# Graph network on one core: units 14 and 15 of each set turned by VectorE in blocks and carried through DRAM

## The chip, the cores and the metric
One core of one Trainium2 chip. The metric is the device time of one execution in microseconds. Three runs of the kernel before took 1857.96, 1860.52 and 1862.22 us; the median is 1860.52.

## The reference
Four graph layers on 4096 nodes with 128 features, each followed by a residual and a layer norm. The change touches only the third, an attention over the whole graph with four heads of 32 features:

```python
q, k, v = [(x @ W + b).reshape(n, H, C) for ...]                  # H = 4, C = 32
attn = einsum('nhc,mhc->hnm', q, k) / sqrt(C)
neg = where(adj == 0, -inf, attn)
e = where(adj == 0, 0, exp(neg - max(neg)))
out = einsum('nhm,mhc->nhc', e / sum(e), v)                       # then gated with x @ Ws + bs
# layer 1: GRU(relu((adj @ x) @ W)), x        layer 2: normalised (adj + I) @ (x @ W)
# layer 4: hyperbolic: maps of x, adj @ xt, maps back
```

## The kernel before
Layers 1, 2 and 4 are products of the adjacency (64 MB) with a 4096 x 128 matrix. The adjacency streams through a ring of 8 slots of 1 MB (`ring`, `load_ring`); L446 is their matmul.

The attention layer works in **chunks** of 512 rows (8 of them, c = 0 to 7), each of four **tiles** of 128 rows, each of two **sets** of 2048 columns. A chunk has thus 8 sets, numbered 0 to 7 here, and a set 16 **units** of 128 columns; the 128 units of a chunk are also its **places** k. For each unit all four heads are handled together. The mask is made in **columns** of 1024 (16 in a chunk, two in a set). The steps:

- SyncE loads half a column of `adj` at a time into one of two landing tiles `adj_in` (`load_mask`, L345). The load of a half waits until GpSimd has used the same half of the column before.
- GpSimd makes -1e30 or 0 of it (`mask_bias`, L1360), at the earliest when VectorE is done with the column four back, six columns ahead of the place counter.
- TensorE makes scores, two matmuls of 512 columns for one head of one column (`scores`, L553), at every even place.
- VectorE scales, adds the mask and takes the minimum in one instruction (`mask`, L1109), at every odd place. The score banks are two, so a score waits for the mask two before it, and a mask of a new column waits for `unit_turned`: TensorE must be past the units that the tile `cols` still holds.
- ScalarE takes the exponent of one head of one set (`exponent`, L807).
- TensorE turns a unit, four 128 x 128 transposes into one of three PSUM banks (`turn_unit`, L580), at every place.
- ScalarE or VectorE copies it to one of 8 slots `turned` (`copy_unit`, L819 or L1124). VECTOR_PLACES, VECTOR_ALSO and VECTOR_NOT say which units VectorE takes (43 of 128), EXP_MOVED where exponents stand between the copies.
- TensorE multiplies it with the values (`attend`, L594), four units at once, seven places behind: the batch after place 3 of a set takes units 12 to 15 of the set before.

Between these lie post steps for the chunk before (`post_steps`: gate, norms and the hyperbolic maps of the next layer) at fixed places, on VectorE, ScalarE and GpSimd. On GpSimd a slot is four places; the norms wait for VectorE's place 77 (the reduction L1185). They exist in chunks 1 to 7, and mask bias calls end in chunk 7 with column 15. Each engine runs its own list in order, and each wait blocks all that is behind it, on SyncE's queue of DMAs too.

Every second set TensorE also turns the finished output of a tile (`turn_out`, L602, after place 6); at places 57 and 65 it does two steps for the chunk before. The next layer's ring loads (`load_ring(2, 0, True)`, L328) stand in SyncE's queue behind the attention's, and four of its slots lie over the first half of `cols`, four over the second.

## Time and profile before

| | |
|---|---|
| median of 3 runs | 1860.52 us |
| profiled execution, its own time | 1859.99 us |
| its span, first to last instruction | 1858.3 us |
| TensorE busy | 1805.1 us, 97% |
| VectorE busy | 1229.1 us, 66% |
| ScalarE busy | 983.0 us, 53% |
| GpSimd busy | 925.3 us, 50% |
| mean granted clock of TensorE | 0.987 |

The shares are averages over four layers. In the adjacency products TensorE and the DMA engines work and the rest mostly waits; the attention runs from about 590 to 1611 us and uses all engines. Each instruction has a start and a duration; TensorE's and VectorE's instructions overlap a little with the next, so what one costs is best read from start to start. Two fp32 records stand for each attend and each ring matmul.

### The profile page before, as it was taken

To read this page: it belongs to the slowest core of one execution; us is meant where nothing else is said; L and a number is where in the kernel's file an instruction comes from. 1 tells how busy PE (TensorE), PEld (TensorE's weight loads), DVE (VectorE), ACT (ScalarE), POOL (GpSimd) and SP (SyncE) were. 2 spreads that over 40 slices of the span, in tenths; PEclk is the share of its full clock that TensorE was granted. 3 is DMA by queue.
4 is the path that set the end of the run, shared out by engine and by line. 5 is a ranking of instruction groups with operands and counts; after the bars stand their busy time and mean duration, and the time that the engine had idled before them with its cause. 6 is when DMAs were issued, how large, how long until landed. Compare 5 with 4: busy or idle time off the path is not lost.

```text
span 1858.3 us, 41304 instructions
## 1 busy us (share of the span) xinstructions
PE 1805.1 (97%) x15504; PEld 1215.9 (65%) x15504; DVE 1229.1 (66%) x2398; ACT 983.0 (53%) x1512; POOL 925.3 (50%) x981
## 2 busy tenths in 40 slices
PE   7999999999996999999999999999999999999996
PEld 3444444444444888888888888888888888644442
DVE  4777775122226888898888888888988889401322
ACT  0111110101004888888888888988888988501101
POOL 0111111111225756778788788787787886540211
PEclk9999999999997999999999999999999999999998
DMA  9867767799977322213222222232133231697781
GB/s 376 303 227 260 256 225 251 270 391 380 400 271 220 93 91 72 83 58 95 88 73 90 74 82 86 70 92 91 60 93 93 64 96 49 242 356 281 281 325 71
DMA packets 110305, 328.82 MB, mean 177 GB/s; under 512 B 13104, under 2 KB 31280, under 8 KB 85552
## 3 DMA queue, kind: packets, MB, share of 16 engines
q1 hardware_dynamic: 87552, 285.25, 43.9%
q10 hardware_dynamic: 20016, 32.78, 4.9%
q0 software_dynamic: 2560, 8.39, 1.6%
q8 instruction: 115, 1.88, 0.4%
q14 instruction: 62, 0.51, 0.1%
HBM read 299.11 MB, written 27.26 MB: 176 GB/s over the span
## 4 chain that ended last, share of the span: by engine, by line
PE 59%; issue 3%; ACT 2%; POOL 2%; DVE 1%; POOLq 0%; DVEq 0%; ACTq 0%
PE bank L580 21%; PE bank L553 13%; PE bank L594 13%; PE bank L446 11%; ACT arena L807 2%; POOL arena L1360 1%; DVE arena L1124 1%; PE bank L434 0%; ACT L858 0%; PE bank L622 0%; PE bank L690 0%; POOL small L1480 0%; ACT arena L819 0%; PE bank L602 0%; POOL small L1367 0%
## 5 line engine op out<-in xcount | busy, mean ns | idle before, releaser
L580 PE MATMUL bank<-ident,arena 128*128 128x128 f32 x4096 | 540.0, 274 | 5.4 <-ACT arena L807 2.4
L580 PEld LDWEIGHTS bank<-ident,arena 128*128 128x128 f32 x4096 | 478.1, 141 | 82.5 <-DVE arena L1124 7.7
L807 ACT ACTIVATE arena<-arena,small 128x2048 f32<-128x2048 f32 x256 | 512.5, 2002 | 0.1
L819 ACT ACTIVATE arena<-bank 128x512 f32<-128x512 f32 x680 | 382.4, 596 | 125.3 <-PE bank L580 123.0
L446 PE MATMUL bank<-arena,stat_s 128*128 128x512 f32 x1008 | 441.4, 595 | 2.1 <-issue 1.2
L553 PE MATMUL bank<-k,parts 128*128 128x512 f32 x1024 | 371.8, 445 | 13.3 <-DVE small L1109 7.0
L446 PEld LDWEIGHTS bank<-arena,stat_s 128*128 128x128 f32 x1008 | 190.2, 191 | 228.3 <-issue 226.9
L1124 DVE COPY arena<-bank 128x512 f32<-128x512 f32 x344 | 236.7, 688 | 73.3 <-PE bank L580 71.6
L1360 POOL TENSOR_SCALAR early<-arena 128x512 bf16<-128x512 f32 x128 | 246.3, 1925 | 68.9 <-DVE small L1109 26.7
L594 PE MATMUL bank<-arena,stat_x 128*32 128x128 f32 x8192 | 276.5, 276 | 0.0
L1360 POOL TENSOR_SCALAR arena<-arena 128x512 bf16<-128x512 f32 x128 | 247.2, 1931 | 40.5 <-DVE small L1109 19.8
L446 PE MATMUL bank<-arena,stat_x 128*128 128x512 f32 x512 | 229.2, 599 | 10.7 <-DMA arena<-adj_cols 8.5
L594 PEld LDWEIGHTS bank<-arena,stat_x 128*32 128x32 f32 x8192 | 208.1, 109 | 42.8 <-issue 42.8
L553 PEld LDWEIGHTS bank<-k,parts 128*128 128x128 f32 x1024 | 155.6, 191 | 68.0 <-issue 44.2
L446 PEld LDWEIGHTS bank<-arena,stat_x 128*128 128x128 f32 x512 | 96.4, 192 | 125.7 <-issue 125.4
L1109 DVE CUSTOM_DVE_ANT_0 arena<-bank,early,small 128x1024 f32<-128x1024 f32 x128 | 163.5, 1279 | 16.6 <-issue 9.3
L1109 DVE CUSTOM_DVE_ANT_0 arena<-bank,arena 128x1024 f32<-128x1024 f32 x128 | 155.9, 1219 | 26.2 <-PE bank L580 20.9
L1109 DVE CUSTOM_DVE_ANT_0 arena<-bank,arena,small 128x1024 f32<-128x1024 f32 x128 | 163.2, 1277 | 6.2 <-issue 5.2
L1109 DVE CUSTOM_DVE_ANT_0 arena<-bank,early 128x1024 f32<-128x1024 f32 x128 | 155.8, 1218 | 15.0 <-PE bank L553 7.8
L1305 POOL TENSOR_SCALAR small<-small 128x4 f32<-128x4 f32 x32 | 13.0, 407 | 251.5 <-DVE small L937 251.5
L1367 POOL TENSOR_TENSOR small<-small 128x4 f32<-128x4 f32 x160 | 78.8, 492 | 60.5 <-DVE small L1185 35.8
L1367 POOL TENSOR_TENSOR arena<-arena 128x512 f32<-128x512 f32 x64 | 76.3, 1192 | 36.4 <-ACT arena L848 20.7
(152 smaller groups left out, 1182.8 us busy)
## 6 DMA issues: line engine op xcount, KB each, us to landing
arena<-adj_cols SPq DMA_DIRECT2D x190, 1024.0 KB, 6.3
arena<-adj SPq DMA_DIRECT2D x256, 256.0 KB, 2.7
k_dram<-arena ACTq DMA_DIRECT2D x32, 256.0 KB, 6.7
q_dram<-arena ACTq DMA_DIRECT2D x32, 256.0 KB, 11.7
k<-k_dram POOLq DMA_DIRECT2D x32, 256.0 KB, 8.5
parts<-q_dram SPq DMA_DIRECT2D x128, 64.0 KB, 2.3
x_dram<-arena ACTq DMA_DIRECT2D x16, 256.0 KB, 3.6
arena<-x_dram ACTq DMA_DIRECT2D x16, 256.0 KB, 4.9
```

The source lines that it names most:

```text
L446: mm_ = pe.matmul(bank[:, to, :], stat[:, jt, :], ring[:, s, j, :], start=(jt == 0), stop=(jt == TILES - 1))
L553: last = pe.matmul(bank[:, u + i, :], parts[:, t % 2, h * P:(h + 1) * P], k4[:, h, at_:at_ + CHUNK], start=True, stop=True)
L580: last = pe.transpose(bank[:, b_, h * P:(h + 1) * P], cols[:, st % SETS, h, u * P:(u + 1) * P], ident[:, :])
L594: last = pe.matmul(bank[h * C:(h + 1) * C, 7, st * P:(st + 1) * P], stat_x[:, k % UPT, h * C:(h + 1) * C], turned[k % TURNED][:, h * P:(h ...
L807: act.activation(cols[:, s_, h, :], cols[:, s_, h, :], ACT.Exp, bias=shift[:, t % 2, 1, i:i + 1], scale=-1.0, accum_out=blocksum[:, t % 2, ...
L819: act.activation(turned[k % TURNED], bank[:, TURN_BANKS.bank(("unit", k)), :], ACT.Copy).then_inc(unit_copied_act, 1)
L1109: dve.tensor_tensor_reduce(out=cols[:, s_, h, hi * BLOCK:(hi + 1) * BLOCK], in0=bank[:, 2 * (h % 2):2 * (h % 2) + 2, :].rearrange("p b n - ...
L1124: dve.tensor_copy(turned[k % TURNED], bank[:, TURN_BANKS.bank(("unit", k)), :]).then_inc(unit_copied_dve, 1)
L1305: step(c, "eps", pool.tensor_scalar(rstd, mean_var[:, :, 1], LN_EPS, None, ALU.add))
L1360: pool.tensor_scalar(maskbias[m % 4][:, e * HALF:(e + 1) * HALF], adj_in[e], 0.0, MASKED, ALU.is_equal, ALU.mult).then_inc(bias_ready, 1)
L1367: step(c, name, pool.tensor_tensor(out_, a, b, op))
```

## The change
Units 14 and 15 of each set (`PAIRS`) are not turned by TensorE. VectorE turns them in 32 x 32 blocks (`turn_blocks`, at places 4 and 7 of the set) into `pair_blocks`, eight tiles of `stat_s`, which the next layer fills only later. SyncE stores the 512 KB to one of two DRAM buffers (`store_pair`) and loads them with four DMAs of 128 KB, which put the blocks in place (`load_pair`), into slots 6 and 7 of the ring of turned units. The attend of such a unit waits for `pair_landed` and reads its operand in runs of 32 elements. The mask loads are named six columns ahead (`MASK_AHEAD`), which places them between the stores and loads of the pairs; the residual loads move to the end of a chunk. VectorE's copies are 32 a chunk, ScalarE's 80, at other places.

```diff
+BLOCK_TURN_AT = {14: 4, 15: 7}
+PAIRS = ((14, 15),)
+VECTOR_PLACES = ()
+VECTOR_ALSO = (0, 4, 8, 11, 13, 16, 20, 23, 24, 34, 54, 58, 64, 67, 73, 83, 85, 86, 88, 90, 92, 98, 102, 104, 105, 106, 113, 115, 118, 121, 123, 125)
...
+MASK_AHEAD = 6
...
+    pair_dram = nc.dram_tensor("pair_dram", [2, P, 2 * CHUNK], F32)
...
+        pair_slot = arena[:, RING + 10 * CHUNK:RING + 12 * CHUNK]
+        pair_blocks = stat_s[:, TILES - 2 * TPC:TILES, :].rearrange("p t f -> p (t f)")
...
                     if first and layer == 2 and s % 4 == 0:
-                        sp.wait_ge(unit_turned, (CHUNKS * SPC - 2 + s // 4 + 1) * UPS)
+                        turned_before = (CHUNKS * SPC - 2 + s // 4 + 1) * UPS
+                        sp.wait_ge(unit_turned, pe_turns(turned_before))
+                        sp.wait_ge(blocks_turned, block_turns(turned_before))
...
+            def store_pair(g):
+
+                i = pairs_until(g)
+                sp.wait_ge(blocks_turned, 2 * (i + 1))
+                if i >= 2:
+                    sp.wait_ge(pair_landed, 16 * (P // C) * (i - 1))
+                sp.dma_start(pair_dram[i % 2, :, :], pair_blocks).then_inc(pair_out, 16)
+
+            def load_pair(g):
+
+                i = pairs_until(g)
+                sp.wait_ge(pair_out, 16 * (i + 1))
+                if i == 0:
+                    sp.wait_ge(gcn_x2_out, 16 * CHUNKS)
+                if g + 1 >= TURNED:
+                    sp.wait_ge(unit_used, g + 1 - TURNED + 1)
+                for j in range(P // C):
+                    sp.dma_start(pair_slot[j * C:(j + 1) * C, :].rearrange("k (q n) -> k q n", q=P // C),
+                                 pair_dram[i % 2, :, j * 2 * P:(j + 1) * 2 * P].rearrange("(q k) n -> k q n", q=P // C)
+                                 ).then_inc(pair_landed, 16)
+
+            def attention_loads(c):
+                for st in range(SPC):
+                    for half_set in range(2):
+                        ahead = c * COLS + 2 * st + half_set + MASK_AHEAD
+                        if ahead < CHUNKS * COLS:
+                            load_mask(ahead // COLS, ahead % COLS, False)
+                        for pair in PAIRS:
+                            if pair[0] // UPB == half_set:
+                                store_pair(c * UPC + st * UPS + pair[0])
+                        if half_set == 1 and st % SETS == 1:
+                            ahead = c * TPC + st // SETS + 2
+                            if ahead < CHUNKS * TPC:
+                                load_queries(ahead // TPC, ahead % TPC, False)
+                        if half_set == 1 and st == 4 and c > 0:
+                            store_x3(c - 1)
+                        for pair in PAIRS:
+                            if pair[0] // UPB == half_set:
+                                load_pair(c * UPC + st * UPS + pair[0])
+                load_residuals(c)
...
+                if is_block_turned(k):
+                    pe.wait_ge(pair_landed, 16 * (P // C) * (pairs_until(c * UPC + k) + 1))
...
-                    turn_unit(c, k, first)
+                    if not is_block_turned(k):
+                        turn_unit(c, k, first)
...
+            def turn_blocks(c, k):
+
+                st, u = k // UPS, k % UPS
+                i = pairs_until(c * UPC + k)
+                dve.wait_ge(exp_ready, (c * SPC + st) * H + H)
+                if i > 0:
+                    dve.wait_ge(pair_out, 16 * i)
+                dve.transpose(pair_tiles(pair_blocks)[:, in_pair(k), :, :, :],
+                              cols[:, st % SETS, :, u * P:(u + 1) * P].rearrange("p h (j k) -> p h j k", j=P // C)
+                              ).then_inc(blocks_turned, 1)
...
+                    if isinstance(c, int) and c == CHUNKS - 2:
+                        pool.wait_ge(pair_out, 16 * CHUNKS * SPC * len(PAIRS))
                     tt("xt", stat_s[:, bass.ds(c * TPC, TPC), :], tiles(mx_g), s1.unsqueeze(2).to_broadcast([P, TPC, P]),
```

`pairs_until(g)`, `pe_turns(g)` and `block_turns(g)` count the pairs, the units turned by TensorE and the block turns before unit g of the layer. On **TensorE**, the last eight places of a set before:

```order
L553 MATMUL bank<-k,parts 128x512 x2
L580 MATMUL bank<-ident,arena 128x128 x8
L553 MATMUL bank<-k,parts 128x512 x2
L580 MATMUL bank<-ident,arena 128x128 x8
L594 MATMUL bank<-arena,stat_x 32x128 x16
```

and the same places now (L618 scores, L645 turns, L667 attend), with the first scores of the next set:

```order
L618 MATMUL bank<-k,parts 128x512 x2
L645 MATMUL bank<-ident,arena 128x128 x8
L618 MATMUL bank<-k,parts 128x512 x2
L645 MATMUL bank<-ident,arena 128x128 x8
L667 MATMUL bank<-arena,stat_x 32x128 x16
L618 MATMUL bank<-k,parts 128x512 x2
L645 MATMUL bank<-ident,arena 128x128 x8
L618 MATMUL bank<-k,parts 128x512 x2
L667 MATMUL bank<-arena,stat_x 32x128 x16
L618 MATMUL bank<-k,parts 128x512 x2
```

The eight turns between the last scores of a set and its last attend are gone. On **SyncE**, in the middle of the layer before (L345 mask halves, L354 queries, L374 and L375 residuals):

```order
L345 DMA arena<-adj 128x512 [waits bias_ready] x8
L354 DMA parts<-q_dram 32x4x128 [waits scores_ready]
L354 DMA parts<-q_dram 32x4x128 x3
L345 DMA arena<-adj 128x512 [waits bias_ready] x4
L374 DMA arena<-x_dram 128x512 [waits att_x3_out,att_pool]
L375 DMA arena<-root_dram 128x512
```

and now, one set of the even kind and one of the odd (L387 mask halves, L406 store of the pair, L417 its loads, L396 queries):

```order
L387 DMA arena<-adj 128x512 [waits bias_ready] x4
L406 DMA pair_dram<-stat_s 128x1024 [waits pair_landed,blocks_turned]
L417 DMA arena<-pair_dram 32x4x256 [waits unit_used,pair_out]
L417 DMA arena<-pair_dram 32x4x256 x3
L387 DMA arena<-adj 128x512 [waits bias_ready] x4
L406 DMA pair_dram<-stat_s 128x1024 [waits pair_landed,blocks_turned]
L396 DMA parts<-q_dram 32x4x128 [waits scores_ready]
L396 DMA parts<-q_dram 32x4x128 x3
L417 DMA arena<-pair_dram 32x4x256 [waits unit_used,pair_out]
L417 DMA arena<-pair_dram 32x4x256 x3
```

Each set's store has four mask halves ahead of it, and the next set's mask halves have the pair's loads ahead of them. On **VectorE**, places 2 to 8 of set 2 before (L1109 masks, L1124 copies, L1142 the weighing of an output):

```order
L1124 COPY arena<-bank 128x512 [waits unit_used,unit_turned]
L1109 ISA arena,small<-bank,early,small 128x1024 [waits masked_ready,scores_ready]
L1109 ISA small 128x1
L1109 ISA arena,small<-bank,early,small 128x1024 [waits masked_ready,scores_ready]
L1109 ISA small 128x1
L1124 COPY arena<-bank 128x512 [waits unit_used,unit_turned]
L1109 ISA arena,small<-bank,arena 128x1024 [waits scores_ready,bias_ready,unit_turned]
L1109 ISA small 128x1
L1142 TENSOR_TENSOR arena<-bank,small 128x256 [waits rows_pe,rows_pool]
```

and now (L1182 masks, L1197 copies, L1206 block turns, L1226 the weighing):

```order
L1197 COPY arena<-bank 128x512 [waits unit_used,unit_turned]
L1182 ISA arena,small<-bank,early,small 128x1024 [waits masked_ready,scores_ready]
L1182 ISA small 128x1
L1206 STREAM_TRANSPOSE stat_s<-arena 128x4x4x32 [waits pair_out,exp_ready]
L1182 ISA arena,small<-bank,early,small 128x1024 [waits masked_ready,scores_ready]
L1182 ISA small 128x1
L1182 ISA arena,small<-bank,arena 128x1024 [waits scores_ready,blocks_turned,bias_ready,unit_turned]
L1182 ISA small 128x1
L1206 STREAM_TRANSPOSE stat_s<-arena 128x4x4x32 [waits pair_out,exp_ready]
L1226 TENSOR_TENSOR arena<-bank,small 128x256 [waits rows_pe,rows_pool]
```

One block turn comes before the mask of place 5, one behind the mask of place 7; the copy of place 6 is gone from VectorE.

## Rows read from the trace of the kernel before

**Rows 1.** Windows (length, then PE, PEld, DVE, ACT, POOL busy): sets 4 to 7, 0

```profile
1038.61:1055.25 16.64, 16.64 (x223) 14.12 (x219) 14.36 (x28) 14.72 (x23) 9.52 (x7) 1.00 0.35 105
1055.25:1070.80 15.55, 15.55 (x213) 13.01 (x209) 14.96 (x26) 13.36 (x19) 12.65 (x20) 1.00 0.12 35
1070.80:1087.46 16.66, 16.22 (x214) 13.09 (x210) 14.19 (x26) 15.43 (x24) 13.65 (x22) 1.00 0.27 81
1087.46:1102.99 15.53, 15.53 (x212) 12.99 (x208) 13.42 (x23) 13.85 (x22) 13.48 (x15) 1.00 0.26 79
1102.99:1119.25 16.26, 16.17 (x215) 13.19 (x211) 13.84 (x26) 13.94 (x21) 13.79 (x12) 1.00 0.40 122
...
sum 127.99, PE 127.45 PEld 106.01 DVE 113.12 ACT 113.14 POOL 101.71; mean PE 15.93 PEld 13.25 DVE 14.14 ACT 14.14 POOL 12.71
```

**Rows 2.** Timeline (start, us, engine, line) of TensorE: places 0 to 3 of set 7

```profile
1086.45 1.08 PE L594 MATMUL bank<-arena,stat_x 128*32 128x128 f32 x32
1087.46 0.73 PE L553 MATMUL bank<-k,parts 128*128 128x512 f32 x2
1088.03 1.03 PE L580 MATMUL bank<-ident,arena 128*128 128x128 f32 x8
1088.82 0.71 PE L553 MATMUL bank<-k,parts 128*128 128x512 f32 x2
1089.37 1.04 PE L580 MATMUL bank<-ident,arena 128*128 128x128 f32 x8
1090.33 1.08 PE L594 MATMUL bank<-arena,stat_x 128*32 128x128 f32 x32
```

**Rows 3.** Timeline of VectorE: a copy and the mask behind it

```profile
1065.64 0.68 DVE L1124 COPY arena<-bank 128x512 f32<-128x512 f32 x1
1066.24 1.21 DVE L1109 CUSTOM_DVE_ANT_0 arena<-bank,early 128x1024 f32<-128x1024 f32 x1
```

**Rows 4.** Timeline of VectorE at place 7 of set 6; TensorE's attend batch then

```profile
1078.89 1.22 DVE L1109 CUSTOM_DVE_ANT_0 arena<-bank,arena 128x1024 f32<-128x1024 f32 x1 [0.84 <-PE bank L580]
1080.04 0.42 DVE L1142 TENSOR_TENSOR arena<-bank,small 128x256 f32<-128x256 f32 x1
...
1078.69 1.08 PE L594 MATMUL bank<-arena,stat_x 128*32 128x128 f32 x32
```

**Rows 5.** SyncE's DMAs: queries, to landing; then x_dram, to landing

```profile
L354 SPq DMA_DIRECT2D parts<-q_dram x120: 327/432/1577, 606.1 to 1528.8; - x120
...
DMA to landing us min/median/max: 1.9/2.3/3.9
...
DMA to landing us min/median/max: 2.8/3.3/4.7
```

**Rows 6.** Landing times of mask halves (256 KB), then of ring slots (1 MB)

```profile
DMA to landing us min/median/max: 2.5/2.7/4.6
...
DMA to landing us min/median/max: 4.7/6.7/12.1
```

**Rows 7.** Timeline of GpSimd: the norms, then biases of sets 5, 6, 7, 0

```profile
1055.09 1.04 POOL L1367 TENSOR_TENSOR small<-small 128x4 f32<-128x4 f32 x1 [5.00 <-DVE small L1185]
...
1060.23 3.94 POOL L1360 TENSOR_SCALAR arena<-arena 128x512 bf16<-128x512 f32 x2 [0.25 <-POOL small L1367]
...
1080.11 3.94 POOL L1360 TENSOR_SCALAR early<-arena 128x512 bf16<-128x512 f32 x2 [0.25 <-POOL small L1367]
...
1096.46 3.94 POOL L1360 TENSOR_SCALAR arena<-arena 128x512 bf16<-128x512 f32 x2 [0.25 <-POOL small L1367]
...
1109.94 3.93 POOL L1360 TENSOR_SCALAR early<-arena 128x512 bf16<-128x512 f32 x2 [0.25 <-POOL stat_s L1367]
```

**Rows 8.** Timeline of TensorE: place 8 of the layer's last set; the next product

```profile
1604.08 2.00 PE L580 MATMUL bank<-ident,arena 128*128 128x128 f32 x16
...
1610.93 3.70 PE L446 MATMUL bank<-arena,stat_s 128*128 128x512 f32 x8
```

More of the change, by code:

```diff
@@ L100, in __call__, with is_block_turned, pe_turns, pairs_until @@
         return c * len(self.names) + self.names.index(name) + 1
+def is_block_turned(k):
+    return k % UPS in BLOCK_TURN_AT
+PE_UNITS = [k for k in range(UPC) if not is_block_turned(k)]
+def pe_turns(g):
+    return g // UPC * len(PE_UNITS) + sum(k < g % UPC for k in PE_UNITS)
+def pairs_until(g):
+    return g // UPS * len(PAIRS) + sum(pair[-1] < g % UPS for pair in PAIRS)
+def block_turns(g):
+    return g // UPS * len(BLOCK_TURN_AT) + sum(u < g % UPS for u in BLOCK_TURN_AT)
+def in_pair(k):
+    return [pair.index(k % UPS) for pair in PAIRS if k % UPS in pair][0]
 class TurnBanks:
@@ L111, in __init__ @@
         for k in range(UPC):
-            self.uses.append(("unit", k))
+            if not is_block_turned(k):
+                self.uses.append(("unit", k))
             if k % UPT == OUT_AT:
@@ L141 @@
 LAST_BLOCK_CHUNK = CHUNKS - BLOCK // CHUNK
-BY_VECTOR = [k for k in range(UPC) if (k % 16 in VECTOR_PLACES or k in VECTOR_ALSO) and k not in VECTOR_NOT]
-BY_SCALAR = [k for k in range(UPC) if k not in BY_VECTOR]
+BY_VECTOR = [k for k in PE_UNITS if (k % 16 in VECTOR_PLACES or k in VECTOR_ALSO) and k not in VECTOR_NOT]
+BY_SCALAR = [k for k in PE_UNITS if k not in BY_VECTOR]
 EXP_PLACES = [EXP_MOVED.get(k, k) for k in range(1, UPC, 4)]
@@ L356, in load_queries @@
                                  ).then_inc(q4_landed[t % 2], 16)
-            def attention_loads(c, first):
-                for m in range(COLS):
-                    if m % BLOCKS == 0:
-                        load_queries(c, m // BLOCKS, first)
-                    if not (first and m == 0):
-                        load_mask(c, m, first)
-                    if m == 5 and not first:
-                        load_residuals(c - 1)
-                    if m == 15 and not first:
-                        store_x3(c - 1)
@@ L372, in load_residuals @@
+            def load_residuals(c):
+                if c == 0:
+                    sp.wait_ge(gcn_q_out, 64 * CHUNKS)
+                    sp.wait_ge(gcn_root_out, 16 * CHUNKS)
+                    sp.wait_ge(gcn_x2_out, 16 * CHUNKS)
+                else:
                     sp.wait_ge(att_pool, AG(c - 1, "h"))
@@ L1211, in attention @@
                         below_max(c, k // UPT)
+                    for u, place in BLOCK_TURN_AT.items():
+                        if k % UPS == place:
+                            turn_blocks(c, k - place + u)
                     if k in BY_VECTOR:
```

55 lines of the change are left out of this document (27 added, 28 removed).

## The prediction
> **What bounds the kernel now.** I read the table of windows first, one window for each set of the middle chunks. TensorE is busy in 127.45 of 127.99 us of a chunk at full clock; VectorE has 113.12, ScalarE 113.14, GpSimd 101.71 [rows 1]. So in the attention layer (eight such chunks of the 1858.3 us span) TensorE is the bound and the other two stand at 88%. Then the timeline of TensorE, which repeats every 3.88 us: two scores, 8 turns, two scores, 8 turns, one attend batch [rows 2]. From the second 8 turns to the attend is 0.96 us, the attend batch 1.01 us, a pair of scores 0.54 to 0.57 us, and a plain set 4 x 3.88 = 15.5 us. A turn is thus 0.11 to 0.12 us of TensorE. Last I read VectorE around place 7 of a set, GpSimd from place 77 to the end of a chunk, and the landing times of SyncE's transfers, because the new transfers wait in SyncE's queue behind mask loads, which wait for GpSimd.
>
> **What TensorE loses.** Units 14 and 15 of each of 64 sets are no longer turned: 8 turns a set. Bounds: 0.79 us (the first 8 turns of a period) to 0.96 us (the second) [rows 2]; I take 0.93, since the removed ones stand where the 0.96 is. That is 7.4 us a chunk, 59.5 in all (51 to 62), if nothing else is late.
>
> **VectorE and ScalarE.** VectorE makes 32 copies a chunk instead of 43 and 16 block turns; ScalarE 80 copies instead of 85, so it only gets lighter. A copy holds VectorE for 0.60 us, start to start [rows 3]. No block turn is in the trace. It moves as many elements (512 a partition) as a copy, so I take 0.65, just above that row; the ends are 0.5 and 1.15, the mask of 1024 elements [rows 4]. VectorE: 113.1 - 11 x 0.60 + 16 x 0.65 = 116.9 us, against 119.5 that TensorE would need (below). It fits on the whole but not in each set: set 6 goes from 14.19 to 15.5 (five copies stay, two turns come), set 7 from 13.42 to 15.3 (one copy more, two turns), where a set of TensorE is 14.6 to 15.0. In the other sets copies go where the turns come. I charge about 1 us a chunk for this.
>
> The Trainium skill (VectorE: DVE Perf Modes, The three transpose paths) gives 311 ns for a 128x128 bf16 block turn; four of them would be 1.24 us, an estimate by that page. Its DVE Microarchitecture page (The reshape front-end and per-opcode configuration) says the transposing array keeps one element per cycle per lane, which would put it at the copy. No run here shows either; my sum goes by the copy, and the slow case is a rival below.
>
> **The round trip of the pair.** Store 512 KB, wait, load 4 x 128 KB. Rows: 256 KB to and from DRAM land in 3.3 us, mask halves of 256 KB in 2.7, queries of 64 KB in 2.3, ring slots of 1 MB in 6.7 among others and 4.7 at best [rows 5, 6]. From 2.7 to 4.7 is 2.0 us for 768 KB more, so 256 KB more cost 0.65 and the store 3.3 + 0.65 = 3.95. The four loads issue 0.43 us apart, so the last is out after 1.3 us and lands 2.4 later (between 64 and 256 KB): 3.7. With 0.4 for two semaphores and the transfers beside: 8.1 us. Bounds: (2.8 + 0.65) + (1.0 + 1.9) = 6.4 with each at its best, (4.7 + 0.65) + (1.3 + 3.9) + 0.2 = 10.7 with each at its slowest [rows 5].
>
> The time it has: the mask of place 7 begins at 1078.89 and lets the next instruction go at 1080.04; TensorE's place 8 began at 1078.69 + 1.01 = 1079.70. So the block turn of place 7 ends 0.34 + 0.65 = 1.0 us into place 8 [rows 4]. Place 8 to place 16 is 7.76, less 0.93; from place 16 to the attend batch 2.87, and unit 14 stands in its middle, 0.5 later [rows 2]. That gives 6.83 + 3.37 - 1.0 = 9.2 us, against 8.1. In a plain set the trip is hidden with 1.1 us to spare.
>
> The Trainium skill (DMA: Bandwidth & Descriptors, Anatomy of one DMA) puts a transfer at 2.0 us plus bytes over 436 GB/s. For 256 KB that is 2.6 us; the mask half's 2.7 agrees [rows 6], the 3.3 of the transfers with DRAM buffers does not [rows 5]. By the rule the trip would be some 7 us and the waits below 1 us a trip shorter.
>
> **The step I think decides: SyncE's order.** Its queue is now, for each set, mask load of column 2s+6, mask load of column 2s+7, store, pair loads. The second half of the load of column 2s+7 waits until GpSimd has finished both halves of the bias of column 2s+6. In the kernel before such a load could be late at no cost; now the store stands behind it. Where does GpSimd finish that bias, counted from the start of the set on TensorE? Set 5 (start 1055.25): 1064.2, 8.9 us in, just in time, for VectorE's turn ends 9 to 10 us in. Set 6 (start 1070.80): 1080.11 + 3.94 = 1084.05, 13.3 us in. Set 7 (1087.46): 1100.40, 12.9 us in. Set 0 (1102.99): 1113.87, 10.9 us in [rows 1, 7]. GpSimd hardly idles from 1055.09 on, where the norms of place 77 begin after a wait of 5.0 us for VectorE; from there to the end of set 6's bias are 29.0 us of its own work, and that does not shrink.
>
> One chunk after, time from the start of set 4: sets 4, 5, 6 take 15.7, 14.6 and 15.0 (before less 0.93; set 6 also loses waits, [rows 1]). Norms begin at 16.5, set 6's bias is done at 45.5, the store goes at 45.9, the pair is there at 54.0. TensorE wants it at 15.7 + 14.6 + 15.0 + 3.4 = 48.7: it waits 5.3 us, in set 7. Next: bias of set 7 done at 61.8, pair at 70.3, wanted at 45.3 + 5.3 + 14.6 + 3.4 = 68.6: 1.7 us more. Set 0's bias, at 75.3, is then earlier than VectorE's turn. So 7.0 us a chunk. The wait also lets VectorE catch up in sets 6 and 7. The eight sets less 0.93 each, without the old waits of sets 6 and 0 (1.1), are 119.5; 119.5 + 7.0 + 0.5 = 127.0, a gain of 1 us, with a little taken for the uneven start 1.3. This holds for chunks 1 to 6. Chunk 0 has no post steps on GpSimd, chunk 7 loads no masks from set 5 on: 7.4 - 1 = 6.4 each.
>
> **Edits priced at nothing.** Mask loads named six columns ahead still find only two landing tiles, so they run one column ahead of GpSimd as before; after the pair loads the even column's load goes out some 14.9 us into a set and lands 2.7 later, 3 us into the next. In sets 5 to 0 GpSimd comes to it later than that; in sets 3 and 4 it may be ready before, and its 5.0 us of waiting ahead of the norms take that up [rows 7]. Query loads, the residual loads and the store of x3 sit in the 4 us in which SyncE waits for the store anyway; each has over 10 us until it is wanted. The attend of a block-turned unit reads runs of 32 elements and not 128: same number of columns, taken at the same 1.01 us a batch (a slower read would show in that batch). The wait of GpSimd in the last chunk for all stores stands ahead of nothing that TensorE wants before the sixth slot of the next layer.
>
> **The end of the layer.** The next layer's product starts at 1610.93 with its first four slots loaded since the second last set was turned [rows 8]. Now its loads stand behind the last pair. Place 8 of the last set is at 1604.08 [rows 8]; with no mask ahead of it the last block turn is done by about 1603.8. The store lands at 1607.9, the loads are out by 1609.6, the two residual loads by 1610.4, then slot 0 of 1 MB takes 4.7 to 6.7 [rows 6]. The product starts at 1615.1 to 1617.1 instead of 1610.0 (a set's 0.93 less): 6 us lost (3 to 9). Later slots come faster (2.6 us a MB) than TensorE takes them (8 records in 3.7 us).
>
> **Sum.** 6 x 1.3 + 2 x 6.4 - 6 = 14.6 us faster. The profiled execution took 1859.99 us (span 1858.3 and 1.7 around it), 0.5 less than the median of the runs, 1860.52. So 1859.99 - 14.6 = 1845.4, with the half microsecond to the median 1846 us. Own range of this case 1830 to 1862: a microsecond in the round trip moves it by some 1.5 us a chunk.
>
> **Rivals.**
> A. SyncE's order costs nothing, because GpSimd runs ahead when TensorE is late, or the trip is short. For it: GpSimd has 101.7 us of work in 127. Against: it is without a pause exactly where the store waits. Then 59.5 - 8 (VectorE) - 6 = 45.5: 1814.5, as a run 1815 us.
> B. The block turn costs 1.15 us instead of 0.65: VectorE has 125 us a chunk, with its issue gaps about 127, and is the bound: 8 x 1 - 6 = 2, so 1858 us. For it: the page's figure. Against: nothing in these rows.
> C. Slower. The trip outlasts its 9.2 us in every set, so place 3 of each set waits. It decides from 9.2 us on, and the gain is gone from about 9.5. At 10 us, six plain sets pay 0.8 each (4.8) and the two late ones 7.5: 131.8 us a chunk, 3.8 more than now. 6 x 3.8 = 23, chunks 0 and 7 gain 1 each, and the end costs 6: 27 slower, 1887 us; with every transfer at its slowest 1925. For it: transfers of one set overlap mask and query loads. Against: the medians leave 1.1 us.
>
> **Chances.** Forecast 0.47, A 0.17, B 0.11, C 0.25. A difference under 0.2% (1856.8 to 1864.2) can't be told from none. Of the forecast's case four fifths lie below that band and an eighth in it; A is all faster; B is half in it; C is slower. Faster 0.58, same 0.11, slower 0.31. The range goes from A's time to C's at 10 us, a microsecond beyond each: 1814 to 1888.
>
> **What would show it.** TensorE's attend batch at place 3 of a set waits for a transfer: about 5 us in set 7, 2 in set 0, nothing in sets 2 to 5. The store's issue follows the mask load at once in sets 6 and 7, and VectorE's turn elsewhere. Block turn 0.65 us (B: over 1). Store plus loads 8.1 us (C: over 9.2, a wait in all sets). The ring loads start after the last pair load. I am wrong if place 3 waits nowhere, or everywhere.

## The result, and the profile after

| | before | after |
|---|---|---|
| median of the runs | 1860.71 us (6 runs) | 1874.44 us (6 runs, 1871.91 to 1882.83) |
| profiled execution | 1859.99 us, span 1858.3 | 1871.91 us, span 1870.2 |
| mean granted clock of TensorE | 0.987 | 0.982 |

The kernel became slower: the ratio is 1.0082, with an interval of 1.0060 to 1.0104. The forecast was 1846 us, so the direction was missed. The range of 1814 to 1888 held the time, but the forecast's own range ended at 1862; the wider one reached up to the time of a rival whose cause did not occur.

The windows of sets 4 to 7 and 0 of a middle chunk of the kernel after, with the columns of [rows 1]:

```profile
1168.10:1184.34 16.24, 16.00 (x214) 13.11 (x210) 15.01 (x29) 14.61 (x23) 11.15 (x8) 1.00 0.40 130
1184.34:1199.01 14.67, 14.67 (x204) 12.06 (x200) 14.32 (x25) 13.91 (x23) 11.77 (x20) 1.00 0.49 155
1199.01:1214.57 15.56, 15.31 (x206) 12.17 (x203) 14.93 (x30) 14.64 (x21) 12.71 (x21) 1.00 0.29 90
1214.57:1234.69 20.12, 16.37 (x205) 13.13 (x201) 15.29 (x26) 12.56 (x18) 17.53 (x18) 0.92 0.48 154
1234.69:1252.02 17.33, 15.31 (x207) 12.20 (x203) 14.65 (x28) 13.04 (x18) 12.24 (x10) 1.00 0.51 162
```

Set 5 is 0.9 us shorter than before (14.67 for 15.55), set 6 1.1. Set 7 is 4.6 us longer, and in it the granted clock is 0.92, GpSimd busy for 17.53 us. Set 0 is 1.1 longer.

Inside set 7, the timeline of TensorE at places 2 and 3, to be read beside [rows 2]:

```profile
1215.93 0.71 PE L618 MATMUL bank<-k,parts 128*128 128x512 f32 x2
1216.47 1.03 PE L645 MATMUL bank<-ident,arena 128*128 128x128 f32 x8
1217.44 0.64 PE L667 MATMUL bank<-arena,stat_x 128*32 128x128 f32 x16
1221.83 1.08 PE L667 MATMUL bank<-arena,stat_x 128*32 128x128 f32 x16 [3.75 <-DMA arena<-pair_dram]
1222.84 1.22 PE L618 MATMUL bank<-k,parts 128*128 128x512 f32 x2
1223.86 1.65 PE L645 MATMUL bank<-ident,arena 128*128 128x128 f32 x8
1225.27 0.70 PE L618 MATMUL bank<-k,parts 128*128 128x512 f32 x2
```

The batch stops after units 12 and 13 and waits 3.75 us for the pair. Behind the wait the same instructions take longer: scores 1.22 for 0.71 us, eight turns 1.65 for 1.03, the half batch 1.08 for 0.64. The windows of these stretches give the clock, the third column from the right:

```profile
1221.83:1225.20 3.37, 3.37 (x25) 2.66 (x26) 1.00 (x1) 0.24 (x1) 2.83 (x5) 0.51 0.38 120
1225.20:1230.66 5.46, 5.46 (x65) 4.53 (x63) 4.50 (x10) 5.27 (x9) 4.67 (x6) 1.00 0.21 57
```

The granted clock is 0.51, the lower level of 1.2 GHz, for these 3.4 us, then 1.00 again. It costs half the stretch, about 1.7 us, on top of the wait.

Why the pair is late: SyncE's queue, and the biases of GpSimd (start, us), in the same sets; they answer to [rows 7]:

```profile
1197.75 1.74 SPq L417 DMA_DIRECT2D arena<-pair_dram  x4
1200.73 12.84 SPq L387 DMA_DIRECT2D arena<-adj  x4
1213.67 0.38 SPq L406 DMA_DIRECT2D pair_dram<-stat_s  x1
1217.63 1.75 SPq L417 DMA_DIRECT2D arena<-pair_dram  x4
...
1198.75 3.95 POOL L1447 TENSOR_SCALAR arena<-arena 128x512 bf16<-128x512 f32 x2 [0.25 <-POOL small L1454]
1209.27 3.94 POOL L1447 TENSOR_SCALAR early<-arena 128x512 bf16<-128x512 f32 x2 [0.25 <-POOL small L1454]
1218.38 3.92 POOL L1447 TENSOR_SCALAR early<-arena 128x512 bf16<-128x512 f32 x2 [0.25 <-POOL arena L1454]
```

The four mask halves leave over 12.84 us, the last when GpSimd's bias of 1209.27 ends at 1213.21. The store is out 0.46 later, the loads 3.96 behind it, and the pair is there at 1221.83.

VectorE's block turn, beside the copy and mask of [rows 3, 4]:

```profile
1595.53 0.68 DVE L1197 COPY arena<-bank 128x512 f32<-128x512 f32 x1
1596.13 0.70 DVE L1206 STREAM_TRANSPOSE stat_s<-arena 128x512 f32<-128x512 f32 x1
1596.76 0.38 DVE L1226 TENSOR_TENSOR arena<-bank,small 128x256 f32<-128x256 f32 x1
```

It holds VectorE 0.63 us, start to start; a copy 0.60.

The end of the layer, to be read with [rows 8]:

```profile
1612.89 1.52 PE L667 MATMUL bank<-arena,stat_x 128*32 128x128 f32 x48
1618.66 1.08 PE L667 MATMUL bank<-arena,stat_x 128*32 128x128 f32 x16 [4.25 <-DMA arena<-pair_dram]
1623.22 5.99 PE L511 MATMUL bank<-arena,stat_s 128*128 128x512 f32 x8 [3.48 <-DMA arena<-adj_cols]
```

The last pair comes 4.25 us late, the first ring slot 3.48 later still, and the first eight records of the product take 5.99 us for 3.70. From the start of the layer's last set to the product are 20.65 us, 13.28 before.

**Where the time went.** Differences between the two profiled executions, beside the terms of the prediction, in us; the 0.9 that the last set was to gain stands with the end (6 - 0.9), where it was measured:

| part | predicted | measured |
|---|---|---|
| chunk 0, to its end | -6.4 | -1.0 |
| chunks 1 to 6 | -7.8 | +7.7 |
| chunk 7, sets 0 to 6 | -5.5 | -1.8 |
| last set and end of the layer | +5.1 | +7.4 |
| the rest | 0 | -0.4 |
| sum | -14.6 | +11.9 |

The six chunks took 128.1, 129.5, 128.3, 131.2, 129.8 and 129.3 us, 129.4 in the mean, against 128.0 to 128.4 before. In set 7 TensorE waited for the pair 3.84, 4.26, 1.66, 3.75, 3.87 and 2.76 us, in set 0 0.34 to 1.77: 4.5 a chunk. The low clock followed in set 7 of all but the third of them, and in set 1 of chunk 0 behind a wait of 2.45.

### The profile page after: what moved, and what is told of

It reads as the page before. It is cut to its first block and busy times, and to the rows that moved or that the text cites. A ratio compares the mean times of both kernels' runs of the same rounds, so it can differ in the third digit from the quotient of the medians.

```text
span 1870.2 us, 40787 instructions
## 1 busy us (share of the span) xinstructions
PE 1767.1 (94%) x14992; PEld 1160.7 (62%) x14992; DVE 1253.1 (67%) x2438; ACT 965.8 (52%) x1472; POOL 925.4 (49%) x981
## 5 line engine op out<-in xcount | busy, mean ns | idle before, releaser
L645 PE MATMUL bank<-ident,arena 128*128 128x128 f32 x3584 | 481.6, 275 | 7.7 <-DVE arena L1226 7.3
L645 PEld LDWEIGHTS bank<-ident,arena 128*128 128x128 f32 x3584 | 422.3, 142 | 79.3 <-DVE arena L1226 14.5
L891 ACT ACTIVATE arena<-bank 128x512 f32<-128x512 f32 x640 | 358.2, 598 | 115.4 <-PE bank L645 112.5
L618 PE MATMUL bank<-k,parts 128*128 128x512 f32 x1024 | 375.2, 449 | 15.2 <-DVE small L1182 8.5
L667 PE MATMUL bank<-arena,stat_x 128*32 128x128 f32 x8192 | 284.1, 278 | 38.2 <-DMA arena<-pair_dram 38.1
L667 PEld LDWEIGHTS bank<-arena,stat_x 128*32 128x32 f32 x8192 | 208.1, 110 | 99.4 <-issue 49.2
L1197 DVE COPY arena<-bank 128x512 f32<-128x512 f32 x256 | 173.5, 686 | 49.6 <-PE bank L645 49.0
L618 PEld LDWEIGHTS bank<-k,parts 128*128 128x128 f32 x1024 | 156.8, 193 | 72.3 <-issue 44.0
L1182 DVE CUSTOM_DVE_ANT_0 arena<-bank,arena,small 128x1024 f32<-128x1024 f32 x128 | 161.1, 1277 | 22.0 <-issue 21.0
L1182 DVE CUSTOM_DVE_ANT_0 arena<-bank,early,small 128x1024 f32<-128x1024 f32 x128 | 162.0, 1275 | 12.8 <-PE bank L618 7.7
L1182 DVE CUSTOM_DVE_ANT_0 arena<-bank,arena 128x1024 f32<-128x1024 f32 x128 | 155.1, 1217 | 19.9 <-PE bank L645 9.8
L1182 DVE CUSTOM_DVE_ANT_0 arena<-bank,early 128x1024 f32<-128x1024 f32 x128 | 154.9, 1215 | 5.5 <-PE bank L618 5.2
L1206 DVE STREAM_TRANSPOSE stat_s<-arena 128x512 f32<-128x512 f32 x128 | 90.2, 705 | 0.0
## 6 DMA issues: line engine op xcount, KB each, us to landing
arena<-pair_dram SPq DMA_DIRECT2D x256, 128.0 KB, 2.8
```

The source lines that it names most:

```text
L618: last = pe.matmul(bank[:, u + i, :], parts[:, t % 2, h * P:(h + 1) * P], k4[:, h, at_:at_ + CHUNK], start=True, stop=True)
L645: last = pe.transpose(bank[:, b_, h * P:(h + 1) * P], cols[:, st % SETS, h, u * P:(u + 1) * P], ident[:, :])
L667: last = pe.matmul(to, stat_x[:, k % UPT, h * C:(h + 1) * C], weights, start=(u == 0), stop=(u == UPS - 1))
L891: act.activation(turned[k % TURNED], bank[:, TURN_BANKS.bank(("unit", k)), :], ACT.Copy).then_inc(unit_copied_act, 1)
L1182: dve.tensor_tensor_reduce(out=cols[:, s_, h, hi * BLOCK:(hi + 1) * BLOCK], in0=bank[:, 2 * (h % 2):2 * (h % 2) + 2, :].rearrange("p b n - ...
L1197: dve.tensor_copy(turned[k % TURNED], bank[:, TURN_BANKS.bank(("unit", k)), :]).then_inc(unit_copied_dve, 1)
```

## The experiments

Two theories stood at the start. One is the prediction's: the pair is late because SyncE's queue makes its store wait for mask loads, and these for GpSimd. The other: it is late because of VectorE's turn, or the trip itself. Times are medians, each ratio is to the kernel before with its 95% interval; the kernel after stands at 1874.44 us. Lines headed by what waits and for what are totals of waits (us, times, longest) from 700 to 1560 us.

**e1_store_first.** The store ahead of the mask load of the odd column.

```diff
-                        if ahead < CHUNKS * COLS:
-                            load_mask(ahead // COLS, ahead % COLS, False)
...
                                 store_pair(c * UPC + st * UPS + pair[0])
+                        if ahead < CHUNKS * COLS:
+                            load_mask(ahead // COLS, ahead % COLS, False)
```

> Only SyncE's order changes: in each set the store of the pair stands ahead of the mask load of column 2s+7, not behind it. Theory Q (the store is late because it queues behind a mask load that waits for GpSimd): the store goes when VectorE's second block turn is done in all sets, the pair loads of sets 6 and 7 are at most half a microsecond late, set 7 falls from about 20.1 us to 15, set 0 by about 1.5, and the stretches at half clock behind those waits go too: about 7 us a chunk in chunks 1 to 6, so 1828 to 1838 us. Rival T (store plus loads are simply longer than the time they have): the waits in sets 7 and 0 stay, above 1860 us.

Measured: 1903.0 us, 1.0229 (1.0201 to 1.0258). The expectation failed.

```profile
SPq L406 <- DVE stat_s L1206: 283.8, 52, 9.6
...
POOL early L1447 <- DMA arena<-adj: 62.4, 25, 6.5
...
PE bank L667 <- DMA arena<-pair_dram: 31.7, 17, 4.2
```

The store now waits for VectorE's turn at the head of the queue, 283.8 us (32.5 in the kernel after), and the mask load behind it goes out late. GpSimd waits 62.4 us for mask halves ahead of the biases into `early` and 84.8 in all, for 67.6 in all in the kernel after, and VectorE waits for GpSimd's post steps in set 2, which takes 17 to 19 us for 15.35. The coupling was turned round, not removed, and TensorE waits 31.7 us for the pair as in the kernel after (31.4).

**e2_mask_last.** Store, pair loads, and only then the odd column's mask load.

```diff
-                        if ahead < CHUNKS * COLS:
+                        if half_set == 0 and ahead < CHUNKS * COLS:
...
                                 load_pair(c * UPC + st * UPS + pair[0])
+                        if half_set == 1 and ahead < CHUNKS * COLS:
+                            load_mask(ahead // COLS, ahead % COLS, False)
```

> SyncE's order again: store, pair loads, and only then the mask load of column 2s+7. Theory Q: no wait for the pair in any set. If GpSimd has slack enough, the time is that of the variant with the store first, 1828 to 1838 us. Rival P (GpSimd is the hidden bound): its column 2s+7 now comes late in every set, it waits for mask halves, the masks of VectorE come late in sets 6 and 7, and the time is 5 to 20 us above the variant with the store first.

Measured: 1966.58 us, 1.0576 (1.0556 to 1.0596). From 700 to 1560 us TensorE waits for no pair any more (one wait of 3.9 us is left, at the end of the layer), and the masks became the bound:

```profile
PE bank L621 <- DVE small L1185: 62.1, 20, 6.8
...
POOL arena L1450 <- DMA arena<-adj: 65.5, 16, 8.7
...
DVE small L1005 <- POOL arena L1457: 46.1, 6, 8.2
```

The expectation's rival, late masks and a late GpSimd, had the kind and was far too low in size. The masks have no slack to give to the pair.

**e3_turn_early.** The block turns at places 2 and 5 instead of 4 and 7.

```diff
-BLOCK_TURN_AT = {14: 4, 15: 7}
+BLOCK_TURN_AT = {14: 2, 15: 5}
```

> VectorE's block turns at places 2 and 5 of a set in place of 4 and 7. SyncE's order stays. Theory Q: the store of sets 6 and 7 waits for GpSimd, not for VectorE, so set 7 stays near 20.1 us. The even sets lose the 0.5 us that the weighing behind the turn of place 7 costs: 4 x 0.5 x 8 = 16 at most, so 1860 to 1868 us. Rival T: the trip starts 1.8 us earlier, so the wait in set 7 falls from 3.8 to 2.0 and that in set 0 goes: 1845 to 1855 us.

Measured: 1872.22 us, 1.0058 (1.0036 to 1.0080).

```profile
SPq L406 <- DVE stat_s L1206: 2.0, 3, 0.8
...
PE bank L667 <- DMA arena<-pair_dram: 32.5, 20, 4.8
```

The store no longer waits for VectorE (2.0 us for 32.5), and TensorE waits for the pair as long as before (32.5 for 31.4). So VectorE's turn is not what makes the pair late. A by-product: sets 2, 3, 4 and 6 fall by 0.3 to 0.45 us (set 2 from 15.35 to 15.05). In the kernel after TensorE waits 26 times for the weighing (L1226), 6.4 us, and 7 times for the normalising in VectorE's post steps (L1018), 3.9 us; the turn at place 7 stands just ahead of the weighing. In e3 neither wait is left.

**e4_no_trip.** Neither store nor loads; the attend reads VectorE's tile as it stands, so the blocks are not in their places and the output is not the reference's. The turn, which waited for the store before, now waits until TensorE has used the pair before (not in the cut below).

```diff
             def store_pair(g):
-                sp.dma_start(pair_dram[i % 2, :, :], pair_blocks).then_inc(pair_out, 16)
+                return
...
-                    pe.wait_ge(pair_landed, 16 * (P // C) * (pairs_until(c * UPC + k) + 1))
+                    pe.wait_ge(blocks_turned, 2 * (pairs_until(c * UPC + k) + 1))
...
-                        weights = pair_tiles(pair_slot)[:, in_pair(k), h, :, :]
+                        weights = pair_tiles(pair_blocks)[:, in_pair(k), h, :, :]
```

> No store and no loads of the pair: the attend of units 14 and 15 reads VectorE's block-turned tile directly, so its blocks are not in their places and the output is not the reference's. It prices what is left without the trip. Theory Q plus VectorE's price as the sets without a wait show it (14.66 odd, 15.35, 15.88, 16.24, 15.57 the even ones and set 3): about 122.8 us a chunk in place of 128.0, no late ring loads: 1815 to 1822 us. Rival B (VectorE's turns are the bound): above 1850 us.

Measured: 1838.15 us, 0.9885 (0.9866 to 0.9905), some 20 us above what was expected. Chunks 0 and 1 were near the forecast; from chunk 2 on set 2 took 17.4 to 19.3 us instead of 15.35, and a chunk 125.7 to 127.7.

```profile
DVE small L989 <- POOL arena L1441: 22.0, 6, 4.6
```

In set 2 VectorE waits for GpSimd's post steps, 4.6 us at most. A second bound was hidden under the first: GpSimd, whose post steps VectorE needs (e6 tests it).

**e5_light_pool** and **e6_no_trip_light.** The kernel after, and e4, with a GpSimd whose biases cost 1.07 us a half instead of 1.93, because from chunk 1 on they make only half of the mask (the output is not the reference's).

```diff
-                    pool.tensor_scalar(maskbias[m % 4][:, e * HALF:(e + 1) * HALF], adj_in[e], 0.0, MASKED,
-                                       ALU.is_equal, ALU.mult).then_inc(bias_ready, 1)
+                    width = HALF if is_zero(c) else HALF // 2
+                    pool.tensor_scalar(maskbias[m % 4][:, e * HALF:e * HALF + width], adj_in[e][:, 0:width], 0.0,
+                                       MASKED, ALU.is_equal, ALU.mult).then_inc(bias_ready, 1)
```

> The changed kernel with less work on GpSimd: from chunk 1 on each mask bias call handles 256 of its 512 columns (the other half keeps an older bias, so the output is not the reference's). Order and transfers are the same. Theory G (GpSimd's late bias holds the store in SyncE's queue, and GpSimd's chain is the second bound): set 7 falls from 20.1 us to 15, set 0 to 15.4, no half clock behind them: about 123 us a chunk in chunks 1 to 6, 1825 to 1840 us. Rival T (the round trip itself is too long): set 7 stays at 19 or more, 1865 to 1875 us.

> Both at once: no round trip (the attend reads the block-turned tile) and half the mask bias on GpSimd; output not the reference's. Theory G: the 17.5 to 18.8 us of set 2 in the kernel without the trip are VectorE waiting for GpSimd's blend; they fall to 15.4, a chunk to about 123, and the time from 1838 to 1815 to 1824 us. Rival V (VectorE's own work makes set 2 long): no change, 1833 to 1841 us.

Measured: e5 1842.83 us, 0.9906 (0.9878 to 0.9934); e6 1817.38 us, 0.9764 (0.9744 to 0.9783). e6 is where its theory had it, e5 3 us above its bounds and far from the rival.

```profile
PE bank L667 <- DMA arena<-pair_dram: 6.1, 6, 2.0
```

With the whole trip in place but a lighter GpSimd, the wait for the pair in e5 is 6.1 us instead of 31.4, and set 7 takes 14.9 to 15.2. The waits fall by 25.3 us, and one stretch of low clock is left of five in chunks 1 to 6; at about 1.6 us each that makes 31.7 by estimate, and the whole gain is 31.6. In e6 every middle chunk takes 123.1 to 123.4 us. That is the kernel's speed without pair waits, and 3.2 above the 120.0 that the prediction had for it (119.5 and 0.5).

**e10_before_light.** The control: the same lighter biases in the kernel before, same diff.

> Control: the kernel before, with the mask bias on GpSimd computed over half its width from chunk 1 on (output not the reference's), as in the run with light biases of the kernel after. Theory G (GpSimd's lateness costs only where the pair's store or the masks wait for it, that is in the kernel after): the kernel before had 0.5 and 0.6 us of waits in set 6 and set 0 of a chunk that led back to masks, so at most 7 x 1.1 = 8 us go: 1852 to 1860 us. Rival H (the light biases gain as much in any kernel, some 30 us as in the kernel after, so that run said nothing of the pair): about 1830 us.

Measured: 1857.37 us, 0.9981 (0.9969 to 0.9993). It is worth 0.19% there, 3.5 us, and 31.6 us in the kernel after (1874.44 less 1842.83). A chunk takes 127.4 us there instead of 128.0. GpSimd's lateness was nearly free before and is paid where the pair stands behind it in the queue.

**e7_act_store.** ScalarE issues the store, at place 10, past SyncE's queue.

```diff
-                                store_pair(c * UPC + st * UPS + pair[0])
...
+                    if k % UPS == STORE_AT:
+                        store_pair(c * UPC + k - STORE_AT + PAIRS[0][0])
```

> The pair's store is issued by ScalarE at place 10 of the set; mask loads, queries and pair loads stay in SyncE's queue in the same order. Theory G: the store no longer waits for the mask loads; in sets 6 and 7 the pair loads still wait for them until 13.7 us into the set, which is just in time. Set 7 falls from 20.1 to 15 to 16 us, but GpSimd's blend then holds set 2 (16 to 18 us): 1840 to 1852 us. Rival: ScalarE, held by the wait at place 10 and 0.4 us of issue a set, becomes late: above 1870 us.

Measured: 1873.35 us, 1.0063 (1.0043 to 1.0083); missed. Set 7 fell to 15.1 to 16.0 in chunks 1 to 6, and set 0 rose to 18.4 to 22.8 from chunk 2 on.

```profile
1090.05 9.59 SPq L388 DMA_DIRECT2D arena<-adj  x4
1099.68 2.46 SPq L397 DMA_DIRECT2D parts<-q_dram  x4
1102.24 1.80 SPq L410 DMA_DIRECT2D arena<-pair_dram  x4
...
1095.34 3.94 POOL L1447 TENSOR_SCALAR arena<-arena 128x512 bf16<-128x512 f32 x2 [0.25 <-POOL small L1454]
...
SPq L408 <- PE bank L657: 129.2, 34, 6.2
...
POOL early L1447 <- DMA arena<-adj: 40.3, 24, 7.2
POOL arena L1447 <- DMA arena<-adj: 30.7, 16, 5.8
```

The pair loads still sit in SyncE's queue. The rows are sets 7 and 0 of a middle chunk: the store of set 7 has left at 1096.03, but its loads stand behind four mask halves that wait for GpSimd's bias (done at 1099.28) and behind the query loads, so they go out at 1102.24, and TensorE waits 2.77 us at place 3 of set 0. It is the same coupling, one set later and at the loads instead of the store. SyncE also waits longer for TensorE to free the pair's slots (129.2 us for 58.4), but GpSimd waits for masks hardly longer than in the kernel after (71.0 us for 67.6), so late masks do not explain the stall.

**e8_ring_early.** The first two ring slots of the next layer ahead of the last set's pair.

```diff
+                    if c == CHUNKS - 1 and st == SPC - 1:
+                        load_ring(2, 0, True, EARLY_SLOTS)
...
-            load_ring(2, 0, True)
+            load_ring(2, 0, True, SLOTS, EARLY_SLOTS)
```

> The kernel after, with one edit at the end of the attention layer: SyncE loads the first two ring slots of the next layer before the last set's masks, store and pair loads, and the other six behind them. In the kernel after, the next product starts 20.65 us after the start of set 63 on TensorE, 13.28 in the kernel before; of the 7.4 us between, 4.25 are the wait for the last pair, 3.48 the wait for the first ring slot behind it. Theory E (the end of the layer costs because the ring loads stand behind the last pair): the second wait goes, and part of the time at the lower clock behind it: 3.5 to 5 us less than the kernel after, 1869 to 1871 us. Rival R (the two early megabytes delay the last pair by as much as they save, since both share the same DMA engines): within 1.5 us of the kernel after, 1873 to 1876 us, with the wait for the pair in set 63 grown from 4.25 to about 8 us. The sets before 63 are as in the kernel after in both.

Measured: 1876.64 us, 1.0081 (1.0059 to 1.0103). The time points to the rival, the trace does not:

```profile
1623.16 1.08 PE L670 MATMUL bank<-arena,stat_x 128*32 128x128 f32 x16 [4.11 <-DMA arena<-pair_dram]
1624.17 6.18 PE L514 MATMUL bank<-arena,stat_s 128*128 128x512 f32 x8
```

The last pair's wait stays (4.11), the wait for the ring slot is gone, and the product starts 16.94 us after the last set instead of 20.65: 3.7 gained. They were lost in the attention, whose last set began at 1607.23 instead of 1602.57, with the same code up to there and a mean granted clock of 0.975 for 0.982. The six runs of the kernel after lie 10.9 us apart among themselves, so a gain of 3.7 at the end can't be read from the time of the whole; it is read from the trace.

**e11_half_turn.** e6 with VectorE's block turn over half the elements.

```diff
+                heads = H if is_zero(c) else H // 2
-                dve.transpose(pair_tiles(pair_blocks)[:, in_pair(k), :, :, :],
+                dve.transpose(pair_tiles(pair_blocks)[:, in_pair(k), 0:heads, :, :],
```

> The run without the trip and with light biases, and VectorE's block turns cut from 512 to 256 elements a partition from chunk 1 on (output not the reference's). That run took 1817.4 us with chunks of 123.1 to 123.4 us, where the prediction had 119.5 for TensorE alone plus 1 for VectorE. Theory V (the 3.6 us beyond are VectorE's: scores' masks and weighing wait behind the block turns in the even sets): 16 turns cheaper by about 0.3 us each let chunks fall by 1 to 2.5 us, 1800 to 1810 us. Rival W (what is left is TensorE's own, its periods saving 0.87 and not 0.93 us, and ScalarE's copies): chunks stay within 0.3 us of 123.2, 1815 to 1818 us.

Measured: 1812.84 us, 0.9736 (0.9719 to 0.9752): between the two.

```profile
L1194 DVE STREAM_TRANSPOSE stat_s<-arena 128x256 f32<-128x256 f32 x112 | 49.4, 441 | 4.7 <-PE bank L654 4.6
```

A half turn takes 441 ns for 705, 4.2 us less of VectorE a chunk, and a chunk falls from 123.2 to 122.4. Part of the 3.2 is thus VectorE's; this run shows 0.8, and twice that for the whole turn would be 1.6, an estimate.

**e9_all.** What helped, put together: store from ScalarE at place 8, turns at places 2 and 5, GpSimd's blend a slot earlier, two ring slots early.

```diff
-BLOCK_TURN_AT = {14: 4, 15: 7}
+BLOCK_TURN_AT = {14: 2, 15: 5}
+EARLY_SLOTS = 2
+STORE_AT = 8
...
-                return {4: beta_terms, 6: residual_terms, 9: blend, 11: rs, 14: x3sq, 17: mx_terms, 19: norms,
+                return {4: beta_terms, 6: residual_terms, 8: blend, 11: rs, 14: x3sq, 17: mx_terms, 19: norms,
```

> Four edits together: the store from ScalarE (place 8), block turns at places 2 and 5, GpSimd's blend one slot earlier (before a mask bias), and the first two ring slots of the next layer loaded ahead of the last pair. Theory G: waits in sets 7, 0 and 2 mostly gone, the product of the next layer 5 us earlier: 1818 to 1835 us, below the kernel before. Rival: GpSimd's total chain (its mask loads come behind the pair loads) still holds the chunk at 126 us or more: 1845 to 1860 us.

Measured: 1852.75 us, 0.9950 (0.9930 to 0.9969): it beats both kernels, by less than expected. Sets 2 to 5 take 15.1, 15.4, 15.8 and 14.7 us, but set 0 17.2 to 21.3 from chunk 2 on. As in e7, the pair loads of set 7 stand behind mask halves that wait for GpSimd: in a middle chunk these leave from 1083.95 to 1093.55, the pair loads at 1096.32.

```profile
SPq L409 <- PE bank L660: 110.6, 42, 5.9
...
PE bank L660 <- DMA arena<-pair_dram: 24.9, 12, 3.7
```

**e12_act_both.** e9, with the pair loads on ScalarE too.

```diff
+                    if k % UPS == LOAD_AT:
+                        load_pair(c * UPC + k - LOAD_AT + PAIRS[0][0])
```

> The combination that beat both kernels at 1852.75 us (store issued by ScalarE at place 8, block turns at places 2 and 5, blend in slot 8, two early ring slots), and now the four pair loads are issued by ScalarE too, at place 13 of the set, so that no pair transfer stands in SyncE's queue behind a mask load, and no mask load behind a pair. The combination still had sets 0 at 17 to 21 us and sets 7 at 16 to 18, with pair loads behind mask loads. Theory S (what was left of the loss is the coupling in SyncE's queue): sets 7 and 0 fall to 15 to 16 us in chunks 1 to 7, chunks to 123 to 125, 1828 to 1840 us. Rival T (GpSimd is the second bound by itself: as soon as TensorE is faster than 125 us a chunk, masks come late whoever issues the pair): chunks 126 to 128, 1845 to 1855 us. Rival U (ScalarE's five issues a set and its wait for the store cost it what it has not: copies late, TensorE waits for ScalarE in each set): above 1860 us.

Measured: 1901.16 us, 1.0216 (1.0195 to 1.0238). The time is rival U's, above 1860, but TensorE waits for the pair and hardly for copies, so none of the three has the cause. SyncE's coupling did go: GpSimd waits 31.2 us in all for `adj`, for 67.6 in the kernel after. But the loads come late:

```profile
1118.20 0.34 ACTq L878 DMA_DIRECT2D pair_dram<-stat_s  x1
...
1127.29 2.01 ACT L857 ACTIVATE arena<-arena,small 128x2048 f32<-128x2048 f32 x1 [1.80 <-DVE small L1185]
1127.35 3.12 ACTq L889 DMA_DIRECT2D arena<-pair_dram  x4
```

They leave 9.15 us behind the store, where SyncE needed 3.96. ScalarE reaches its place 13 only behind exponents, one of which waits for a mask. TensorE waits for the pair 32 times, 41.3 us, from 700 to 1560 us, and 7.5 and 11.9 us at the end of the layer. An earlier place for the loads was not tried.

## Why the prediction was wrong

**Right: the path by which the pair comes late, nearly to the microsecond.** From the start of set 4 the prediction had the bias of set 6 done at 45.5, the store out at 45.9, the pair there at 54.0. Measured: 45.1, 45.6 and 53.7; the trip took 8.16 us for 8.1. The pair was wanted at 50.0 and not 48.7, because the three sets ahead took 46.5 us and not 45.3, so the wait was 3.75 and not 5.3. Bias of set 7 done at 61.5, forecast 61.8. The marks held in kind: waits in set 7 (1.66 to 4.26, forecast about 5), smaller ones in set 0 (0.34 to 1.77, forecast 2), the ring loads behind the last pair load. One held in part: 24 of the 53 stores from 700 to 1560 us waited for VectorE's turn, the store of set 5 in the chunk shown did not. e3, e5 and e10 together show the cause: not VectorE's turn and not the length of the trip, but GpSimd through the mask loads. The stall was forecast at 7.0 a chunk; it measured 4.5, and with the clock 5.9.

**Right: the turns and the size of the block turn.** Plain sets such as set 5 became 0.87 us shorter (15.54 to 14.67), forecast 0.93, inside its bounds. The block turn was 0.63 from start to start, forecast 0.65. Rival B is out. Its 1.24 us was four times the 311 ns of the Trainium skill (VectorE: DVE Perf Modes, The three transpose paths), and the multiplication was the mistake: 256 elements take 0.441 us (e11) and 512 take 0.705, which is 1.03 ns an element and some 0.18 us that is paid once; continued to 128 elements, that is 0.31, an estimate, and the page's figure. That the transposing array keeps one element per cycle per lane, as the Trainium skill has it (Vector Engine (DVE) Microarchitecture Reference, The reshape front-end and per-opcode configuration), fits a turn of 0.705 beside a copy of 0.686. The prediction's other rule, 2.0 us plus bytes over 436 GB/s, stands on its page (the Trainium skill, DMA: Bandwidth & Descriptors, Anatomy of one DMA) as a fit for DMAs that GpSimd issues. These were SyncE's, and by the rule the trip came to some 7 us, for 8.16 measured.

**Failed: what a chunk costs apart from the waits.** The prediction had 120.0 us: 8 x 0.93 and the old waits off, and 0.5 of VectorE's price back (its text charges about 1, its sum 0.5). e6, in which nobody waits for the pair, measures 123.2, and sets 2 to 5, in which the kernel after does not wait either, have the same lengths there. Of the 3.2, 8 x 0.06 = 0.5 is the smaller saving. The rest is that sets 1 to 4, 6 and 7 gain only 0.2 to 0.6 us each and not 0.87: set 3 goes from 16.11 (e10) to 15.88. The budget said that 117 us of VectorE fit in 119.5; but a turn in front of a weighing delays TensorE at that place, whatever the sum. e11 puts 0.8 on half of the turns' length; e3 takes back 0.3 to 0.45 in each of four sets by their places alone. What is left of the 3.2 is not assigned. Six chunks of 3.2 are 19 us, the largest term of the 26.5 by which the forecast was off. The smaller stall gives 6 x 1.1 = 6.6 back, which is luck: the sets that were longer than forecast also made the waits shorter. With a few unassigned microseconds the six chunks are 15.5 off.

**Failed: nothing was set down for the clock.** Six waits of 2.45 us and more in the attention each brought 3.4 us at a granted clock of 0.5, which cost 1.5 to 1.7; five lie in chunks 1 to 6, some 8 us together. At the end of the layer the clock was low for 10.2 us, from 1.0 before the wait of 4.25 ended, through the wait of 3.48, into the product. The product's first records are slower for it, but what follows its start is not longer than before (the rest, -0.4).

**Failed: chunks 0 and 7.** They were to gain 6.4 each, for lack of post steps or masks. Chunk 0 gained 1.0: one wait of 2.45 in set 1, with the clock behind it, took 4.4 (19.1 for 14.67, as e6 has it), and its first score came 1.0 us later than before (591.13 for 590.13). Chunk 7 gained 1.8 up to its last set, where 5.5 were forecast; its set 0 took 17.15 us for 15.35, because the stalls of chunk 6 reach into it.

**Mis-sized: the end of the layer,** 8.3 for 6 (20.65 after the last set's start against 13.28 less 0.93). The store left 6.3 us into the last set, forecast 6.15. But the ring loads went out 14.1 in and not 12.75, since the second residual load held the queue for 1.43 us, and slot 0 took 6.5 to come, near the upper end of the 4.7 to 6.7. e8 shows that 3.7 of the loss are the ring's place in the queue.

**The rivals.** A (the order costs nothing) would be e6, which also has no late ring loads, for which A counts 6 us. Even there the time is 1817 and not 1815 with the lighter GpSimd, 1838 with the real one (e4): GpSimd by itself then holds a chunk at 125.7 to 127.7 us. C has the sign, not the cause: of 38.1 us of waits for the pair, 34.0 lie in sets 7 and 0, in set 1 of chunk 0 and at the end of the layer, where C has them in every set.

## What to carry to other kernels

A transfer put in an in-order queue inherits every wait ahead of it and hands its own to all behind: changing the order (e1, e2) or one of the issuers (e7) moved the stall and did not remove it, so give a dependent round trip a queue whose other entries do not wait for the same engines, and a place at which the issuer really is when the data is ready (e12). A budget of busy time does not show an added instruction's price where it stands just ahead of one that the bound engine waits for: read the places, not the sum. And a wait of some microseconds on TensorE can cost more than its length, since a stretch at the lower clock may follow. Its length does not decide that alone: in the kernel after all waits from 2.45 us on were followed by one, but in other runs waits of 1.75 (e1) and 1.98 us (e5) were too, and waits of 2.88 (e7), 3.19 (e12) and 3.22 (e4) were not.

## What the runs showed of the hardware

- In the kernel after, TensorE's granted clock fell to 0.5 for 3.4 us at the end of waits of 2.45 to 4.26 us and for 10.2 us around the two waits at the end of the layer (4.25 and 3.48), and stayed at 1.00 behind waits of 1.77 and less. This is no rule for the length of a wait: it fell after 1.75 us in e1 and stayed at 1.00 after 3.22 in e4.
- A 128x512 fp32 transpose in 32x32 blocks takes 0.705 us on VectorE, 128x256 0.441: nearly what a copy takes from PSUM (0.686).
- A store of 512 KB to DRAM and the loads of 4 x 128 KB back: 3.96 us from the store's issue to the loads' (1213.67 to 1217.63), and 4.2 more until TensorE went on, 8.16 in all.
- Issuing a pair load took a median of 0.43 us on SyncE (the kernel after) and 0.45 on ScalarE (e12).
